# High digits of the cell index written by ScalarE, one fused low-digit operation on VectorE, and the norm step one tile earlier

## The reference

```python
h = tok(x)                                     # (32, 313, 128)
h = h + attn(layernorm(h))                     # softmax(x x^T) x, per clip
h = h + ffn(layernorm(h))

def ffn(hidden):                               # 8 heads of 64, 64 keys for each half, top 16
    q = layernorm(hidden @ Wq.T + bq) * ln_g + ln_b
    s0 = l2norm(q[..., :32]) @ l2norm(keys0).T
    s1 = l2norm(q[..., 32:]) @ l2norm(keys1).T
    sc0, ix0 = top_k(s0, 16); sc1, ix1 = top_k(s1, 16)
    cs = sc0[..., :, None] + sc1[..., None, :]   # 256 sums per head
    ci = ix0[..., :, None] + ix1[..., None, :]   # index 0 .. 126
    fs, pos = top_k(cs, 16); fi = take(ci, pos)
    w = softmax(fs)
    inner = hidden . expert_down[fi]
    return sum(gelu(inner) * w * expert_up[fi])
```

## Time and profile before

| | before |
|---|---|
| time, median of 3 runs | 2131.66 us (2131.37 to 2132.61) |
| profiled execution | 2132.51 us, span 2130.3 us |
| mean granted clock of PE | 0.729 of full speed |

### The profile page before, as it was taken

The page is one execution under the profiler, slowest core; times in us unless marked ns, Lnnn a source line. Parts: engine busy times, 40 slices in busy tenths (PEclk is TensorE's granted clock), DMA queues, the critical chain, the costliest instruction groups (busy, mean ns, idle before and its releaser), DMA issues.

```text
span 2130.3 us, 48144 instructions
## 1 busy us (share of the span) xinstructions
PE 1682.7 (79%) x10975; PEld 1311.4 (62%) x10975; DVE 2008.6 (94%) x16198; ACT 1108.1 (52%) x3515; POOL 1578.8 (74%) x3519
## 2 busy tenths in 40 slices
PE   5567698877869887797888779788877988887666
PEld 3336576655747665575766657666665756666455
DVE  3299999999999999999999999999999999999993
ACT  3344555565555556555555555545555564554443
POOL 2237788787778878777887877788787877878775
PEclk9676877677776777768677686867767686776655
DMA  1000000000000000000000000000000000000000
GB/s 34 13 9 2 18 7 13 14 6 18 6 18 6 8 18 8 18 6 19 7 6 18 9 18 6 18 6 6 19 9 16 9 18 6 6 12 9 6 8 9
DMA packets 46676, 24.86 MB, mean 12 GB/s; under 512 B 4955, under 2 KB 46116, under 8 KB 46390
## 3 DMA queue, kind: packets, MB, share of 16 engines
q1 hardware_dynamic: 46390, 21.80, 3.7%
HBM read 11.52 MB, written 10.26 MB: 10 GB/s over the span
## 4 chain that ended last, share of the span: by engine, by line
DVE 68%; PE 14%; POOL 8%; issue 6%; ACT 3%; another core or an unknown queue 0%; SPq 0%; DMA 0%; DVEq 0%; POOLq 0%; ACTq 0%
DVE hrest L1019 10%; DVE alpha L1049 8%; DVE idx L1025 8%; DVE idx L1028 8%; DVE vals L1016 6%; DVE vals L1023 5%; DVE crest L1079 4%; DVE c L1085 4%; PE FB L446 3%; PE FB L437 3%; PE QB L528 3%; DVE top L1082 2%; POOL bw L884 2%; DVE top L1076 2%; DVE beta L1055 2%
## 5 line engine op out<-in xcount | busy, mean ns | idle before, releaser
L528 PE MATMUL QB<-bw,alpha 128*128 128x48 bf16 x5120 | 553.3, 277 | 62.7 <-issue 62.0
L528 PEld LDWEIGHTS QB<-bw,alpha 128*128 128x128 bf16 x5120 | 521.5, 151 | 101.9 <-issue 93.0
L884 POOL TENSOR_TENSOR bw<-beta,wp 128x1024 bf16<-128x1024 bf16 x240 | 503.9, 2129 | 10.3 <-ACT wp L708 9.9
L722 ACT ACTIVATE WD<-QB 32x96 f32<-32x96 f32 x1280 | 307.2, 240 | 91.9 <-PE QB L528 80.4
L1049 DVE TENSOR_SCALAR alpha<-hi 128x1024 bf16<-128x1024 bf16 x640 | 270.0, 493 | 0.0
L480 PE MATMUL SC<-WK,hidT 128*128 128x512 f32 x320 | 225.3, 794 | 38.8 <-ACT hidT L655 23.9
L829 POOL TENSOR_TENSOR ci<-idxf 128x64 f32<-128x64 f32 (+3 forms) x400 | 123.9, 343 | 177.2 <-DVE beta L1055 176.9
L1025 DVE FIND_INDEX8 idx<-vals,sraw 128x8 uint32<-128x64 f32 x1280 | 250.5, 218 | 0.0
L1028 DVE FIND_INDEX8 idx<-vals,hrest 128x8 uint32<-128x64 f32 x1280 | 250.5, 219 | 0.0
L1019 DVE MATCH_REPLACE8 hrest<-vals,sraw 128x64 f32<-128x64 f32 x1280 | 250.2, 209 | 0.0
L1016 DVE MAX8 vals<-sraw 128x8 f32<-128x64 f32 x1280 | 169.2, 209 | 0.0
(11 more groups left out here) (206 smaller groups left out, 4079.9 us busy)
## 6 DMA issues: line engine op xcount, KB each, us to landing
res<-h_scratch SPq DMA_DIRECT2D x80, 64.0 KB, 1.8
xin<-in_x SPq DMA_DIRECT2D x32, 128.0 KB
h_scratch<-h2n SPq DMA_DIRECT2D x32, 128.0 KB
out<-ofin SPq DMA_DIRECT2D x64, 64.0 KB, 1.6
h_scratch<-h2n SPq DMA_DIRECT2D x32, 28.5 KB
out<-ofin SPq DMA_DIRECT2D x16, 57.0 KB
xin<-in_x SPq DMA_DIRECT2D x32, 28.0 KB
xin<-in_x SPq DMA_DIRECT2D x32, 0.2 KB
```

Source lines behind the costliest of these rows:

```text
L528: last = mm(bank[:, 48 * u:48 * u + 48], alpha[:, buf, a, :, 8 * p + u], bwv[:, :, a, :, 8 * p + u], start=(a == 0), stop=(a == 1))
L722: last = A(WD[r, RING[(t - 4) % NT], :, 8 * p:8 * p + 8], blocks[r, :, :, g], ACT.Copy)
L884: last = tt(bw[:, buf, NY * i:NY * i + NY, :], beta[:, buf, :, :], wp[:, buf, i, :].unsqueeze(1).to_broadcast([128, NY, 256]), ALU.mult)
```

## The change

The digits move partly to ACT. In phase 0 of a slot, ahead of `zexp`, ACT waits for `eb_full` and for DVE to be done with the old `hi`, and writes all four copies of `hi` from PSUM in bf16: the value plus 768 minus 0, 32, 64 or 96. Between 512 and 1024 bf16 has a spacing of 4, so writing rounds to the multiple of 4. DVE waits for these, makes `lo` with one operation (EB + 768 - hi) ahead of `alpha`, and compares `hi` with 768 + 4x. DVE's rounding and its three copies are gone.

The norm step moves: `norms` of a pair runs on DVE in slot 4, phase 1, of the pair before, instead of slot 0; POOL's `newton` for `rn` runs in slot 0 between the cells `cs` and the index cells `ci`, instead of behind `bw`.

```diff
-ROUND4 = 1.5 * 2.0 ** 25
+BASE = 768.0
...
@@ ACT
             def slot(k, t, p):
                 n = NT * k + t
+                if p == 0 and exists(k, t, 3):
+                    act.wait_ge(s["eb_full"], n - 2)
+                    after(act, s["alpha_full"], n - 3)
+                    for c in range(NS):
+                        last = A(hi[:, c, :], STE, ACT.Identity, bias=cdig[:, c:c + 1])
+                    last.then_inc(s["his_full"], 1)
                 if p == 0 and exists(k, t, 2):
...
@@ POOL
+                for c in range(NS):
+                    nc.gpsimd.memset(cdig[:, c:c + 1], BASE - float(NY * NX // NS * c))
...
                     cells(cs[:, buf, :, :], vs[:], s["cs_full"])
+                if p == 0 and t == 0 and exists(k, t, 0):
+                    pool.wait_ge(s["seed4_full"], k + 1)
+                    newton(y4[:], xh4[:], na[:], c15[:], s["rn_steps"], 12 * k, rn[:])
...
-                if p == 3 and t == 0 and exists(k, t, 0):
-                    pool.wait_ge(s["seed4_full"], k + 1)
-                    newton(y4[:], xh4[:], na[:], c15[:], s["rn_steps"], 12 * k, rn[:])
...
@@ DVE
                     if digits:
-                        dve.wait_ge(s["eb_full"], n - 2)
-                        V.tensor_scalar(hi[:, 0, :], STE, ROUND4, ROUND4, ALU.add, ALU.subtract
-                                        ).then_inc(s["hi_full"], 1)
-                    if digits:
-                        dve.wait_ge(s["hi_full"], n - 2)
-                        for c in range(1, NS):
-                            last = V.tensor_scalar(hi[:, c, :], hi[:, 0, :], float(NY * NX // NS * c), None, ALU.subtract)
-                        last.then_inc(s["his_full"], 1)
-                        V.tensor_tensor(lo[:], STE, hi[:, 0, :], ALU.subtract).then_inc(s["lo_full"], 1)
-                    if digits:
                         dve.wait_ge(s["his_full"], n - 2)
+                        V.scalar_tensor_tensor(out=lo[:], in0=STE, scalar=BASE, in1=hi[:, 0, :], op0=ALU.add, op1=ALU.subtract
+                                               ).then_inc(s["lo_full"], 1)
                         after(dve, s["quads_full"], 4 * (n - 4))
...
-                            last = V.tensor_scalar(a8[:, :, :, xx, :], h8, float(NY * xx), None, ALU.is_equal)
+                            last = V.tensor_scalar(a8[:, :, :, xx, :], h8, BASE + float(NY * xx), None, ALU.is_equal)
...
-                    if t == 0 and exists(k, t, 0):
-                        norms(k)
+                    if t == NT - 1 and exists(k, t, -1):
+                        norms(k + 1)
```

More of the change, by code:

```diff
@@ L101, in build @@
         cquart = sb("cquart", [128, 1])
+        cdig = sb("cdig", [128, NS])
         c15 = sb("c15", [128, 80])
@@ L238, in build @@
             rn_steps halves_full vs_full cs_full idxf_full ci_full c2_full zexp_full m_full wexp_full zs_full
-            rz_full wz_full y_full st_full w1_full rest1_full w2_full rest2_full w3_full hi_full his_full lo_full
+            rz_full wz_full y_full st_full w1_full rest1_full w2_full rest2_full w3_full his_full lo_full
             beta_full alpha_full bw_full quads_full wd_full ws_steps g_full gd_full fo_full fin_full
```

## The result

| | before, same chip | after |
|---|---|---|
| time, median | 2132.14 us (2131.37 to 2134.57) | 2099.14 us (2096.61 to 2110.38), 4 runs |
| ratio, 95% interval | | 0.985 [0.982, 0.989] |
| profiled execution | 2132.51 us, span 2130.3 us | 2100.36 us, span 2098.2 us |
| mean granted clock of PE | 0.729 | 0.737 |

The account below looks back on a forecast made before the run. DVE bounds the old kernel; after the change ACT's chain sets part of each pair. Parts of 70.7, 23.4, 1.1 and 28.7 give 123.9 against 125.15 us: 17.5 over 14 pairs plus 9 at the ends, 2105 us, range 2088 to 2122.

Parts of the forecast that it names:

- A: From the end of the second `sy` to the digits of slot 0: 70.7 us, set by ACT.
- B: From the digits of slot 0 to the digits of slot 1: 23.4 us, with 1.1 for the rn chain beside `alpha`.
- C: From the digits of slot 1 to the next `sy`, set by DVE: 32.5 us before, 28.7 after.
- The steady part: The 14 repeating pairs: 1.25 us less a pair, 17.5 us in all.
- the ends: First and last pair, where ACT idles: seven tiles gain in full, with one norm step of the start, 9 us.
- ACT sets the end, and DVE waits some 3.5 us, most of it in slot 0: From `sy` to slot 0's digits, ACT's chain of 70.7 us outlasts DVE's 67.2; some waiting is for the variance.
- DVE alone: 67.2: DVE's own path from `sy` to slot 0's digits: 68.5 less 0.7, 0.6 and 1.1, plus 1.1 for norms.
- Three quarters of what DVE sheds comes back as waiting for ACT: Over the whole kernel, most of DVE's saved time returns as waits for ACT, leaving 2105 us.
- DVE stays the bound: Rival: ACT's groups lie in idle time; pair 118.5 us, time taken as 2040 us, chance 0.12.
- With 2 to 3 us to spare: Slot 4: POOL's `n` is ready at 930.41, DVE's norms get there near 933, so no wait.
- The moved norm chain: rn chain, 5.0 us, moves to slot 0: `alpha` in slot 1 falls 1.8 us, slot 0 gives back 0 to 1.8.
- The clock rivals: PE's clock rises, all pairs like the third: 2076 us, chance 0.20; or falls, like the first: 2132, chance 0.12.

Follow-up runs that it names:

- the last run: Kernel with ACT's group ahead of the front work, plus eight MAX8 ahead of slot 4's digit work and DVE's norms in phase 3 there: 2099.1 us.

## Why the prediction was right, and where only its sum was

**The terms held.** The fused `lo` is 417 ns (414 was taken), `alpha` starts 0.33 us after it, the group takes 1.57 us until the digits are there (1.55), slot 4 waits 0.78 us (0.8), slot 2 never, `alpha` in slot 1 is 2.8 (2.8), DVE's norms don't wait for `n` in the steady pairs. The Trainium skill's formula (ScalarE: Activation LUTs, What ACT_TABLE_LOAD costs) gave an estimate of 1.69 us for the group; the measured 1.57 lies near the row of the squares. The three parts came as A 70.2, B 24.0, C 29.0 against 70.7, 24.5, 28.7. The steady part gave 28 us (forecast 17.5) and the ends 4 (forecast 9), so two misses of opposite sign stand in the total. Of the signs that the prediction named, three came out smaller: DVE's busy time fell by 79 us (95 to 125), ACT's grew by 107 (some 120), and the wait for the variance was above 1.5 us in 5 of the 13 pairs (two of three).

**"ACT sets the end, and DVE waits some 3.5 us, most of it in slot 0": wrong in its cause.** ACT was free 69.9 us after `sy` (forecast 70.7), but the wait at `lo` in slot 0 is 0.4 us in the mean, 2.6 at most. In part A DVE waits 2.7 us in all, most of it for the variance and in slot 4. The step that failed is "DVE alone: 67.2". DVE came at 69.8 (70.2 less the 0.4 of waiting). Into DVE's own path belong the waits that it has on the way, 1.3 for the variance and 0.25 and 0.78 for ACT in slots 3 and 4. I had listed them as effects of the group and then left them out of DVE's sum; with them it is 69.5. Measured, the two chains arrive within 0.1 us of each other in the mean; in nine of the 13 pairs DVE comes last, in four ACT, by 0.7 to 2.6 us. The total was right because the chain through ACT was, and because DVE's, taken 2.6 us too short, doesn't reach beyond it: that is luck. Two chains that meet also make the price of the group rise: 7 to 37 us for the first, by the place of the norms, and 100 us for the second.

**"Three quarters of what DVE sheds comes back as waiting for ACT": the size near, the name wrong.** Per pair DVE sheds 4.6 us of busy time, and 2.8 (three fifths) come back as waits, 1.9 for ACT and 0.9 more for the variance. I had put the wait for the variance down to the group. It is 0.6, 1.5 and 1.6 us a pair in three kernels that have no group (0.4 before, 1.3 after), so an earlier DVE alone brings most of it.

**"DVE stays the bound" at 2040** took `alpha` at 2.8 us beside nothing. Without any group on ACT the kernel is at 2092, at 2074 with the norms later and at 2058 with the norm step back. The missing term is POOL, which this rival had as a free engine: its operations last longer where DVE's are dense, one of them by 3.2 us, and its `n` then has DVE wait. **"With 2 to 3 us to spare"** holds for after (2.9 to 3.3 in the steady pairs); without the group DVE comes 3.0 us earlier and `n` 3.2 later, and it waits 2.6.

**The moved norm chain**: -1.8 in slot 1 was measured as -2.0 (in before and in after), +1.1 for DVE's norms as 1.1 to 1.3, but it took 0.8 us more in part A of after. Net it is -1.1 us a pair in before, +0.2 in after and -1.7 with the group earlier: the worth of one edit depends on which chain is late.

**The clock rivals** didn't come: ACT was free 69.1 to 71.7 us after `sy`, between the ends of the forecast's 68.2 to 73.4, at a mean granted clock of 0.737 (0.729 before).

Two things stay open. After's runs spread over 14 us (2097 to 2110) where before's spread over 3, and the profile, of one execution, doesn't say why. And which of DVE and POOL goes on and which stands, below.

## What to carry to other kernels

A wait that DVE has upstream belongs into its own chain before two chains are compared; when both then arrive together, the next piece of work on either costs more than the last, here up to its full length. Look where an engine idles before some other engine's result, and put the added work ahead of that wait, in the program order: with the norm step moved this was worth 27 us, nearly as much as the change, and with the norm step at its old place 1 us, so two edits have to be measured together as well as one by one. And of two engines that slow each other, count the time of both: making one wait for the other moved the cost to the next slot, in both tries.

## What the runs showed of the hardware

DVE's comparisons and POOL's operations slow each other in one of two ways. Either they alternate (`alpha` 2.9 to 4.6 us instead of 2.75, up to 5.8, POOL's small operations 0.41 to 0.5 us instead of 0.27 to 0.35), or the eight comparisons run at full speed and one POOL operation stands for 3.4 to 4 us. In after, POOL and then DVE:

```profile
865.42 3.97 POOL L863 TENSOR_TENSOR vs<-vals,rn 128x256 f32<-128x256 f32 x1
```

```profile
865.61 2.75 DVE L1050 TENSOR_SCALAR alpha<-hi 128x1024 bf16<-128x1024 bf16 x8
```

By the Trainium skill (SBUF — State Buffer, Who interferes with whom) whoever issues first holds the shared ports for the whole instruction and the other blocks. The three norm operations of 2.03 to 2.16 us beside `bw` agree, and so does the first way, as a turn of a whole instruction each. The second way isn't such a turn: a POOL operation stands through eight of DVE's. In before it occurs in none of the 60 slots of twelve pairs (of which 28 have small operations of POOL beside `alpha`), in after in 12 of 60, in the first run without ACT's group in 30. It was so in slot 4 of every steady pair of the four runs with a constant `hi`, never in slot 4 of any other run, and never behind a wait at `lo` (0 of 148, over twelve pairs of every run); the last run, with no wait and still no standing operation, shows that the wait isn't the cause. In all cases seen POOL's operation began within 0.3 us of `alpha`'s first, but so did many that alternated. What decides wasn't found.
